# Reordering the seam between attention and experts in a fused audio tower, with a small clear on Pool between scatters

## The chip, the cores and the metric

The kernel runs on one core of a Trainium2 chip. The metric is the device time of one execution in microseconds (us). Before the change it is 282.87 us, the median of three runs (281.76 to 283.83).

Engines are named as the profile does: PE (TensorE, with PEld for its weight loads), DVE (VectorE), ACT (ScalarE), POOL (GpSimd), and SP, which only starts DMAs here. Each has its own instruction stream; they wait for one another through counting semaphores.

## The reference

Input is 32 sequences of 125 frames with 23 features. Four stages follow, all in float32 (N = 32 x 121 = 3872 tokens of 128 features):

```python
h = tdnn(x)                      # windows of 5 frames, linear to 128, relu, batch norm over all tokens
h = h + attention(layernorm(h))  # 8 heads of 16, per sequence, with a column bias from an edge list
n = layernorm(h)
e = argmax(n @ Wr + br)          # one of 8 experts per token (top 1, so its gate is 1)
out = h + relu(n @ W1[e] + b1[e]) @ W2[e] + b2[e]    # 128 -> 512 -> 128
```

## The kernel before, in words

Attention is a software pipeline over sequences b = 0 to 31, one step t per sequence (`for t in range(B)`), then five more steps t = 32 to 36 (`for t in range(B, STEPS)`) in which the last sequences drain while the first five expert tiles already run. The order is written out by hand, once for each engine. In step t:

- PE computes the scores of t (`scores`), the turned scores of t-1 (`scores_T`), the weighted values of t-2 (`weigh`), turns results (`turn`, `turn_back`) and projects the output of t-4 (`output`).
- ACT takes the exponent of t-1, copies sums and turned tiles (`turned_copy`, `sums_copy`), and scales rows of t-5 (`scaled_rows`, it sets `s_x2`).
- DVE reduces the row maxima, divides (`divided(t-3)`), adds the first residual and squares (`first_sublayer(t-4)`).
- POOL computes the second norm's factor (`rstd2(t-4)`) and, after every fourth sequence, the router's logits (`logits`).

Sequences are grouped by four (g = 0 to 7; group six is sequences 24 to 27). For each group DVE finds each token's expert (`experts`), PE ranks the tokens within their expert (`rank_rows`, small bf16 products into a corner of a PSUM bank named by `rank_bank`), and DVE picks each token's place in the region of its expert (`rows_picked`, `row_places`, which sets `r_pos`; `expert_seen` carries the counts on). Then POOL scatters the 121 rows of each sequence to a DRAM buffer, with an indirect DMA (`scatter_rows(b)`, line 435). `scatter_step(b)` says in which step.

The expert part works on 38 tiles of 128 rows, each of one expert. The first 11 tiles (NT1) hold rows of the first 20 sequences, the other 27 need all rows. SP loads a tile from DRAM (`load_rows`), PE transposes it (`transpose_rows`), ACT copies it (`xgT_copy`, line 564) and copies the expert's W1 next to it (`W1_copy`, line 557), PE makes the first product (`ffn_first`, line 1246), ACT and DVE each make half of the hidden layer (`relu` 572, `ffn_relu` 883), PE the second product (`ffn_second`, line 1236), DVE adds the residual (`finish_rows`, line 873, sets `f_y`), and POOL scatters the tile's rows to the output with an indirect DMA (`scatter_out(s)`, line 442). The first seven of these wait for a tile six further on (`f_y >= s + 7`), and there is one `pool.drain()` after the output of tile 24.

Places that the change touches, by line: `scatter_step` 244, `rank_bank` 258, `scatter_out` 438, POOL's loops 466 to 483, ACT's `W1_copy(0)` behind its loop, DVE's steps 32 to 36, PE's `transpose_rows(0)` and `rank_rows(NG - 2)` there.

Of the kernel before, what the change touches and what calls it, by code (L numbers as in the profile page):

```python
# [15 lines left out]
B, TF, DI = 32, 125, 23  # L16
# [18 lines left out]
NT = (N + E * 127) // 128  # L35
# [7 lines left out]
NG = len(GROUPS)  # L43
# [5 lines left out]
def build(nc, x, tok_W, tok_b, gamma, beta, edge_index, edge_attr, q_w, q_b, k_w, k_b, v_w, v_b, o_w, o_b,  # L49
          eb_w, eb_b, Wr, br, W1, b1, W2, b2, out):  # L50
    with ExitStack() as ctx:
        def sb(name, shape, dt=F32):
            return ctx.enter_context(nc.sbuf_tensor(name, shape, dt))
# [135 lines left out]
        mask = sb("mask", [128, NT], I32)  # L189
        sidx = sb("sidx", [128, NT], I32)  # L190

        xg = sb("xg", [128, RING, ROW])
        xgT = sb("xgT", [128, 2, 128])
        W1_tile = sb("W1_tile", [128, 2, F])
# [49 lines left out]
        def scatter_step(b):  # L244
            g = next(n for n, (b0, nb) in enumerate(GROUPS) if b0 <= b < b0 + nb)
            first, i = ranked(g) + 1, b - GROUPS[g][0]
            return first + (i if first < B else i // 2)

        def has(t, back, n=B):

# [6 lines left out]

        def rank_bank(g):

            return psO if g < NG - 1 else psU  # L260

        def score_half(turned):

# [58 lines left out]
        def _(pool):  # L322
# [108 lines left out]
            def scatter_rows(b):  # L431
                g = next(n for n, (b0, nb) in enumerate(GROUPS) if b0 <= b < b0 + nb)
                pool.wait_ge(r_pos, g + 1)
                pool.wait_ge(s_x2, b + 1)
                pool.indirect_dma_start(region_d, bass.IndirectOffsetOnAxis(pos[0:L, b:b + 1], 0), rows[0:L, b, E:E + ROW], None,  # L435
                                        bounds_check=E * CAP - 1, oob_is_err=False).then_inc(d_early if b < B1 else d_rows, 16)

            def scatter_out(s):
                u = s % RING
                pool.wait_ge(f_si, s + 1)  # L440
                pool.wait_ge(f_y, s + 1)
                pool.indirect_dma_start(out, bass.IndirectOffsetOnAxis(sidx[:, s:s + 1], 0), y_out[:, u, :], None,  # L442
                                        bounds_check=N - 1, oob_is_err=False).then_inc(f_sca[u], 16)

            pool.wait_ge(s_rowid, 1)
            pool.wait_ge(l_rows, 16 * N_ROWS)
# [18 lines left out]
                    rstd2(t - 4)  # L465
            for t in range(B, STEPS):
                if t == B + 3:
                    for b in range(done, B - 6):
                        scatter_rows(b)
                    done = B - 6  # L470
                if has(t, 4):
                    rstd2(t - 4)
                while done < B and scatter_step(done) <= t:
                    scatter_rows(done)
                    done += 1
            for b in range(done, B):
                scatter_rows(b)
            for s in range(NT):
                if s < ALONG + 2:
                    pool.wait_ge(f_y, s + 7)  # L480
                scatter_out(s)
                if s == NT - 14:
                    pool.drain()
# [3 lines left out]
        def _(act):  # L487
# [65 lines left out]
            def W1_copy(s):  # L553
                e = act.value_load(eid[0:1, s:s + 1], min_val=0, max_val=E - 1)
                if s >= 2:
                    act.wait_ge(f_L1, s - 1)
                act.activation(W1_tile[:, s % 2, :], W1_sb[:, bass.ds(e * F, F)], ACT.Identity).then_inc(f_w1, 1)  # L557
                tile_expert[s % 2] = e
# [38 lines left out]
            def turned_copy(b):  # L597

                act.wait_ge(s_OT, b + 1)
                act.activation(oT[:, :], psO[:, 256:256 + L], ACT.Identity).then_inc(s_oT, 1)  # L600
# [22 lines left out]
            for t in range(B):  # L623
                p, even = t // 2, t % 2 == 0
                if t == 0:
                    xT_copy(1, psO)
                if not even and p + 1 < NP:
                    q_copy(p + 1, psB[:, 0, :])
                if even and p > 0 and p + 3 < NP:
                    batch_norm(p + 3)  # L630
                if has(t, 4):
                    turned_copy(t - 4)
                if even:
                    v_copy(p, psB[:, 0, :])
                if has(t, 1):
                    exponent(t - 1)
                if has(t, 2):
                    sums_copy(t - 2)
                if even and p + 3 < NP:
                    h0_copy(p + 3, psB[:, 1, :])  # L640
                if not even and p + 2 < NP:
                    xT_copy(p + 2, psB[:, 1, :])
                if has(t, 5):
                    scaled_rows(t - 5)
                if t == B - 3:
                    act.wait_ge(f_b1, 1)
                    act.activation(b1T[:, :], psB[:, 1, 0:E * FC], ACT.Identity).then_inc(f_b1T, 1)
# [4 lines left out]
            sums_copy(B - 2)  # L652
            scaled_rows(B - 5)
            xgT_copy(1)
            act.wait_ge(r_eid, 1)
            act.wait_ge(l_ffn, 48)
            W1_copy(0)
            for t in range(B, STEPS):
                s = t - B
                if s > 0:  # L660
# [21 lines left out]
        def _(dve):  # L682
# [139 lines left out]
            def rows_picked(g):  # L822

                b0, nb = GROUPS[g]
                dve.wait_ge(r_rank, g + 1)
                dve.tensor_tensor(picked_row[0:L, 0:nb, :], rank_bank(g)[0:L, 384:384 + nb * E].rearrange("p (b e) -> p b e", e=E),
                                  oh_bf[0:L, b0:b0 + nb, :], ALU.mult).then_inc(r_pick, 1)

            def row_places(g):

                b0, nb = GROUPS[g]
                dve.wait_ge(r_pick, g + 1)
                with nc.allow_low_precision("whole numbers"):
                    dve.tensor_reduce(pos[0:L, b0:b0 + nb], picked_row[0:L, 0:nb, :], AX.X, ALU.add).then_inc(r_pos, 1)
# [74 lines left out]
            def experts(g):  # L909

                expert_max(g)
                expert_rank(g)
                expert_onehot(g)
# [72 lines left out]
            for t in range(B, STEPS):  # L986
                s = t - B
                if has(t, 3):
                    dve.wait_ge(s_P, t - 3)
                    divided(t - 3)  # L990
                if t == B + 2:
                    rows_picked(NG - 2)
                    row_places(NG - 2)
                if t == B + 3:
                    dve.wait_ge(s_P, B)
                if has(t, 4):
                    first_sublayer(t - 4)
                if t == B + 4:
                    experts(NG - 1)
                ffn_relu(s, e)  # L1000
                e_next = tile_expert(s + 1)
                if t == B + 2:
                    expert_seen(NG - 2)
                if t == B + 4:
                    expert_seen(NG - 1)
                    rows_picked(NG - 1)
                    row_places(NG - 1)
                ffn_resid(s, e)
                if s > 0:
                    finish_rows(s - 1)  # L1010
                if t == B:
                    experts(NG - 2)
                e = e_next

            def rest_tiles():
# [54 lines left out]
        def _(pe):  # L1070
# [193 lines left out]
            def turn(b):  # L1264

                pe.wait_ge(s_on, b + 1)
                pe.transpose(psO[:, 256:256 + L], on[0:L, :], ident[0:L, 0:L]).then_inc(s_OT, 1)  # L1267
# [25 lines left out]
            for t in range(B):  # L1293
# [68 lines left out]
                if t == B - 1:  # L1362
                    pe.wait_ge(s_kT, NP)
                    pe.wait_ge(s_qs, 2 * NP)
                    pe.wait_ge(s_Vs, NP)
                    transpose_rows(0)

            pe.wait_ge(s_exp, B - 1)
            pe.wait_ge(s_qm, B)
            scores_T(B - 1)  # L1370
            pe.wait_ge(s_OTs, B - 2)
            turn(B - 4)
            pe.wait_ge(s_h1, B - 4)
# [11 lines left out]
            for t in range(B + 1, STEPS):  # L1385
                s = t - B
                e = tile_expert(s - 1)
                if has(t, 3):
                    pe.wait_ge(s_h1, t - 4)
                    pe.wait_ge(s_on, t - 3)  # L1390
                    turn_back(t - 3)
                    output(t - 4)
                if has(t, 2):
                    weigh(t - 2)
                if t == B + 2:
                    pe.wait_ge(s_oT, B - 1)
                    pe.wait_ge(s_OTs, B)
                    rank_rows(NG - 2)
                pe.wait_ge(f_xT, s + 1)
                transpose_rows(s + 1)  # L1400
                if t == B + 3:
                    pe.wait_ge(s_h1, B - 1)
                    pe.wait_ge(s_on, B)
                    output(B - 1)
                ffn_first(s)
                if has(t, 3):
                    if t == B + 2:
                        pe.wait_ge(r_pick, NG - 1)
                    pe.wait_ge(s_OTs, min(t - 1, B))
                    turn(t - 3)  # L1410
                ffn_second(s - 1, e)

            pe.wait_ge(s_h1, B)
# [47 lines left out]
```

## Time and profile before

| | |
|---|---|
| median of three runs | 282.87 us (281.76 to 283.83) |
| the profiled execution | 282.8 us, span 281.1 us |
| PE busy | 247.3 us, 88% of the span |
| DVE, ACT, POOL busy | 180.9, 165.8, 145.6 us |
| mean granted clock of TensorE | 0.951 of full |
| indirect DMAs to the region (L435) | 32, 1083 ns each on POOL |
| indirect DMAs to the output (L442) | 38, 980 ns each on POOL |

The span is measured inside the execution; the other 1.7 us lie around it. A busy indirect DMA on POOL is the time in which POOL makes its descriptors, not the transfer. "Remote", or "another core or an unknown queue" in the chain of waits, stands where an engine started again and the trace shows nothing that released it.

### The profile page before, as it was taken

The numbers are of one execution on the slowest core, as the hardware profiler recorded it, in microseconds if no ns is written. First come the engines' busy times: TensorE is split into PE (matmuls) and PEld (weight loads), VectorE is DVE, ScalarE is ACT, GpSimd is POOL, SyncE is SP. The second block draws the span as 40 slices with busy tenths as digits, with TensorE's granted clock in tenths as the row PEclk, the third lists the DMA queues.
The fourth block names the chain that finished last, engine by engine and source line by source line (L and its number), as shares of the span: only waits on it lengthen the run. The fifth ranks groups of instructions, "written<-read, shape, count | busy, mean of one in ns | idle before, by whom it ended". The sixth has DMA issues, their size and how long they took to land.

```text
span 281.1 us, 8987 instructions
## 1 busy us (share of the span) xinstructions
PE 247.3 (88%) x2852; PEld 207.9 (74%) x2852; DVE 180.9 (64%) x679; ACT 165.8 (59%) x405; POOL 145.6 (52%) x275
## 2 busy tenths in 40 slices
PE   3999689999999999999998986975969559999693
PEld 3855466888887777878776755965969559999693
DVE  3896555678888788787788864663825225564352
ACT  3873355687676776766765664553536226776460
POOL 8001733344587776777776434475143744443444
PEclk9999999999999999999999997799798958999899
DMA  3110599000010111010110135123045423330000
GB/s 114 38 43 0 150 338 266 3 2 2 2 39 20 38 39 37 21 38 20 38 39 25 30 98 151 39 56 89 2 139 144 124 59 89 97 88 21 27 22 0
DMA packets 14462, 18.20 MB, mean 65 GB/s; under 512 B 3992, under 2 KB 10556, under 8 KB 14417
## 3 DMA queue, kind: packets, MB, share of 16 engines
q1 hardware_dynamic: 10976, 11.23, 14.1%
q0 software_dynamic: 3296, 6.00, 7.3%
q8 instruction: 24, 0.39, 0.6%
q10 hardware_dynamic: 144, 0.41, 0.4%
q14 instruction: 22, 0.17, 0.2%
HBM read 10.58 MB, written 7.54 MB: 64 GB/s over the span
## 4 chain that ended last, share of the span: by engine, by line
PE 67%; DVE 8%; issue 7%; another core or an unknown queue 6%; ACT 5%; POOL 3%; DMA 2%; ACTq 2%; POOLq 1%; SPq 0%; DVEq 0%
PE psS L1246 11%; PE psB L1146 9%; PE psS L1162 6%; PE psB L1236 5%; PE psO L1289 5%; PE psS L1172 4%; PE psO L1236 3%; PE psB L1130 3%; PE psU L1279 2%; DVE nmax L944 2%; PE psO L1267 2%; PE psU L1273 2%; PE psB L1152 2%; PE psB L1223 2%
## 5 line engine op out<-in xcount | busy, mean ns | idle before, releaser
L442 POOL DMA_INDIRECT out<-y_out,sidx x38 | 37.3, 980 | 47.1 <-DVE y_out L873 21.9
L1246 PE MATMUL psS<-xgT,W_tile 128*128 128x128 f32 x304 | 45.8, 300 | 2.7 <-ACT W_tile L557 2.6
L883 DVE TENSOR_SCALAR hT<-psS,b1T 128x128 f32<-128x128 f32 x76 | 23.3, 346 | 37.2 <-PE psS L1246 26.0
L944 DVE TENSOR_REDUCE nmax<-psS 121x8 f32<-121x968 f32 x32 | 37.2, 1164 | 14.6 <-PE psS L1172 13.2
L1246 PEld LDWEIGHTS psS<-xgT,W_tile 128*128 128x128 f32 x304 | 42.1, 214 | 3.3 <-issue 1.9
L609 ACT ACTIVATE PT<-psS 121x968 f32<-121x968 f32 x32 | 31.3, 978 | 17.3 <-DVE nmax L944 14.0
L572 ACT ACTIVATE hT<-psS,b1T 128x128 f32<-128x128 f32 x76 | 23.9, 364 | 29.5 <-PE psS L1246 21.3
L435 POOL DMA_INDIRECT region_d<-rows,pos x32 | 34.7, 1083 | 11.7 <-issue 11.4
L557 ACT ACTIVATE W_tile<-W_sb 128x512 f32 x38 | 23.9, 630 | 6.4 <-issue 3.7
L1236 PE MATMUL psB<-W_sb,hT 128*128 x168 | 25.6, 302 | 1.4 <-issue 1.4
L1236 PEld LDWEIGHTS psB<-W_sb,hT 128*128 128x128 f32 x168 | 23.7, 218 | 1.9 <-issue 1.7
L1162 PE MATMUL psS<-kT,qT 32*121 32x121 f32 x512 | 22.3, 288 | 1.3 <-ACT PT L609 0.7
L1236 PE MATMUL psO<-W_sb,hT 128*128 x136 | 19.5, 289 | 4.3 <-issue 4.1
L1162 PEld LDWEIGHTS psS<-kT,qT 32*121 32x121 f32 x512 | 16.5, 179 | 8.7 <-issue 6.2
L1236 PEld LDWEIGHTS psO<-W_sb,hT 128*128 128x128 f32 x136 | 17.6, 202 | 5.1 <-issue 5.0
L614 ACT ACTIVATE OTs<-psO 128x242 f32<-128x242 f32 x32 | 11.9, 373 | 14.2 <-PE psO L1289 13.8
L1289 PE MATMUL psO<-PT,V 121*32 121x121 f32 x512 | 20.3, 277 | 0.0
L422 POOL TENSOR_SCALAR var<-ss 121x1 f32<-121x1 f32 x32 | 6.1, 192 | 26.3 <-DVE sq L936 21.8
L1223 PE MATMUL psB<-ident,xg 128*128 128x128 f32 x38 | 11.4, 301 | 9.3 <-ACT xgT L564 7.2
L1172 PE MATMUL psS<-qm,kT 32*121 32x121 f32 x512 | 19.5, 265 | 0.0
L426 POOL TENSOR_TENSOR rs<-var,minus_half 121x1 f32<-121x1 f32 x32 | 18.0, 563 | 2.7
L957 DVE TENSOR_TENSOR qm<-qT,psU 128x242 f32<-128x242 f32 x32 | 12.9, 403 | 9.0 <-PE psU L1342 9.0
(261 smaller groups left out, 545.0 us busy)
## 6 DMA issues: line engine op xcount, KB each, us to landing
xg<-region_d SPq DMA_DIRECT2D x38, 129.0 KB
W_sb<-in_L_ffn_W SPq DMA_DIRECT2D x1, 2048.0 KB, 9.8
region_d<-pads SPq DMA_DIRECT2D x1, 1032.0 KB, 6.7
out<-y_out,sidx POOLq DMA_INDIRECT x38
b_bc<-in_L_ffn_b SPq DMA_DIRECT2D x1, 512.0 KB, 5.1
region_d<-rows,pos POOLq DMA_INDIRECT x32
xs<-in_x ACTq DMA_DIRECT2D x1, 402.5 KB, 3.5
edge_i<-in_L_attn_edge_index SPq DMA_DIRECT2D x1, 64.0 KB, 3.8
```

Source lines behind the costliest of these rows:

```text
L435: pool.indirect_dma_start(region_d, bass.IndirectOffsetOnAxis(pos[0:L, b:b + 1], 0), rows[0:L, b, E:E + ROW], None, bounds_check=E * CAP - ...
L442: pool.indirect_dma_start(out, bass.IndirectOffsetOnAxis(sidx[:, s:s + 1], 0), y_out[:, u, :], None, bounds_check=N - 1, oob_is_err=False) ...
L557: act.activation(W1_tile[:, s % 2, :], W1_sb[:, bass.ds(e * F, F)], ACT.Identity).then_inc(f_w1, 1)
L572: ins = act.activation(hT[:, s % 2, c * 128:(c + 1) * 128], psS[:, s % 2, c * 128:(c + 1) * 128], ACT.Relu, bias=b1T[:, bass.ds(e * FC + c ...
L609: act.activation(PT[0:L, b % 2, :, :, :], score_half(1), ACT.Exp).then_inc(s_exp, 1)
L944: dve.tensor_reduce(nmax[0:L, :].rearrange("p (j c) -> p j c", c=HB)[:, :, HD + 1:HD + 3], score_half(0), AX.X, ALU.max, negate=True).then ...
L1146: return pe.matmul(bank[:, g * PL:(g + 1) * PL], w[:, g * 128:(g + 1) * 128], xT[:, p % 2, :], start=True, stop=True)
L1162: ins = pe.matmul(psS[0:L, j, a * 128:a * 128 + L], qT[rws, p % 2, a, n0:n0 + L], kT[rws, p % 2, a, n0:n0 + L], start=True, stop=True)
L1172: ins = pe.matmul(psS[0:L, j, 256 + a * 128:256 + a * 128 + L], kT[rws, p % 2, a, n0:n0 + L], qm[rws, a, :], start=True, stop=True)
L1236: ins = pe.matmul(tile_out(s), hT[:, s % 2, c * 128:(c + 1) * 128], W2_sb[:, bass.ds(e * F + c * D, D)], start=(c == 0), stop=(c == FC - 1))
L1246: ins = pe.matmul(psS[:, c // 2 * 2 + s % 2, c % 2 * 128:(c % 2 + 1) * 128], W1_tile[:, s % 2, c * 128:(c + 1) * 128], xgT[:, s % 2, :], s ...
L1289: ins = pe.matmul(psO[j * HB:(j + 1) * HB, a * 128:a * 128 + L], V[0:L, b // 2 % 2, b % 2, a * HG + j, :], PT[0:L, b % 2, j, a, :], start= ...
```

## The change

POOL:

- `scatter_step` gives two rows per step also to a group that begins in step 30, so that sequences 20 and 21 are scattered in step 30, and 22 and 23 in step 31 (before: 20 to 23 in steps 30 to 33).
- Sequences 24, 25 and 26 are scattered in steps 33, 34 and 35 by explicit calls (before: 24 and 25 in step 35, 26 and 27 in step 36). 27 to 31 follow behind the loop (before: 28 to 31).
- A new tile `pause` of 43 columns. Behind each scatter of sequences 27 to 31, and each scatter to the output but for the last three tiles, POOL clears one column of it with a memset. Nothing reads it.

Group six, a step forward: DVE's `experts` and `expert_seen` stand in step 32 ahead of the first tile's hidden layer, its picks in step 33; PE's `rank_rows` in step 33 without its two waits, in the bank of the tiles' second products; the wait for the pick stands ahead of the second product of tile 0.

ACT copies the first tile's W1 in step 31. PE transposes the first tile behind the last turned scores.

```diff
+        pause = sb("pause", [128, NT + 5])
...
-            return first + (i if first < B else i // 2)
+            return first + (i if first < B - 2 else i // 2)
...
-            return psO if g < NG - 1 else psU
+            return psO[:, :] if g < NG - 2 else psB[:, 1, :] if g == NG - 2 else psU[:, :]
...
                 pool.indirect_dma_start(out, ...
+                if s < NT - 3:
+                    pool.memset(pause[:, s:s + 1], 0.0)
...
             for t in range(B, STEPS):
                 if t == B + 3:
-                    for b in range(done, B - 6):
-                        scatter_rows(b)
-                    done = B - 6
+                    scatter_rows(B - 6)
+                    done = B - 5
                 if has(t, 4):
                     rstd2(t - 4)
-                while done < B and scatter_step(done) <= t:
-                    scatter_rows(done)
-                    done += 1
+                if t == B + 1:
+                    scatter_rows(B - 8)
+                if t == B + 2:
+                    scatter_rows(B - 7)
+                    done = B - 6
             for b in range(done, B):
                 scatter_rows(b)
+                pool.memset(pause[:, NT + b - (B - 5):NT + b - (B - 5) + 1], 0.0)
...   (ACT, step B - 1, behind turned_copy)
+                if t == B - 1:
+                    act.wait_ge(r_eid, 1)
+                    act.wait_ge(l_ffn, 48)
+                    W1_copy(0)
...
             xgT_copy(1)
-            act.wait_ge(r_eid, 1)
-            act.wait_ge(l_ffn, 48)
-            W1_copy(0)
...   (DVE, steps B to B + 4)
-                if t == B + 2:
-                    rows_picked(NG - 2)
-                    row_places(NG - 2)
...
                     first_sublayer(t - 4)
+                if t == B:
+                    experts(NG - 2)
+                    expert_seen(NG - 2)
+                if t == B + 1:
+                    rows_picked(NG - 2)
+                    row_places(NG - 2)
...
-                if t == B + 2:
-                    expert_seen(NG - 2)
...
-                if t == B:
-                    experts(NG - 2)
...   (PE)
-                    transpose_rows(0)
...
             scores_T(B - 1)
+            transpose_rows(0)
...
-                if t == B + 2:
-                    pe.wait_ge(s_oT, B - 1)
-                    pe.wait_ge(s_OTs, B)
+                if t == B + 1:
                     rank_rows(NG - 2)
...
                 if has(t, 3):
-                    if t == B + 2:
-                        pe.wait_ge(r_pick, NG - 1)
                     pe.wait_ge(s_OTs, min(t - 1, B))
                     turn(t - 3)
+                if t == B + 1:
+                    pe.wait_ge(r_pick, NG - 1)
                 ffn_second(s - 1, e)
```

## Rows read from the trace of the kernel before

**Rows 1.** The page's strip of TensorE's granted clock, 40 equal slices, tenths.
```profile
PEclk9999999999999999999999997799798958999899
```

**Rows 2.** The chain of waits from 150 us: start us, us, what.
```profile
223.88 4.83 another core or an unknown queue
...
261.96 2.02 another core or an unknown queue
```

**Rows 3.** The timeline, steps 31 and 32: start us, us, engine line operation [idle before].
```profile
164.55 0.98 ACT L609 ACTIVATE PT<-psS 121x968 f32<-121x968 f32 x1 [0.95 <-DVE nmax L944]
...
169.68 0.63 ACT L557 ACTIVATE W_tile<-W_sb 128x512 f32 x1 [0.34 <-issue]
...
170.45 1.13 PE L1246 MATMUL psS<-xgT,W_tile 128*128 128x128 f32 x8 [1.75 <-ACT W_tile L557]
...
173.33 0.18 DVE L791 TENSOR_REDUCE top<-lg 121x4 f32<-121x32 f32 x1
```

**Rows 4.** Busy time by stretch: engines' busy us, then granted clock, DMA share, GB/s.
```profile
172.50:179.00 6.50, 6.44 (x40) 5.81 (x41) 3.83 (x19) 3.01 (x9) 1.85 (x3) 0.50 0.46 116
193.30:196.00 2.70, 0.00 (x0) 0.00 (x1) 0.39 (x3) 0.39 (x2) 1.19 (x2) 1.00 0.35 96
196.00:199.80 3.80, 3.77 (x18) 3.65 (x19) 2.91 (x21) 2.48 (x7) 0.00 (x0) 0.55 0.01 4
...
264.40:267.90 3.50, 3.47 (x17) 3.50 (x18) 2.08 (x9) 2.23 (x7) 1.95 (x2) 0.51 0.03 9
```

**Rows 5.** The timeline, the scatters of sequences 26 to 31, first and last.
```profile
186.93 1.09 POOL L435 DMA_INDIRECT region_d<-rows,pos  x1 [0.64 <-issue]
...
190.82 0.27 PE L1223 MATMUL psB<-ident,xg 128*128 128x128 f32 x1
...
193.78 1.02 POOL L435 DMA_INDIRECT region_d<-rows,pos  x1 [0.31 <-issue]
...
195.61 0.28 ACT L564 ACTIVATE xgT<-psB 128x128 f32<-128x128 f32 x1 [2.72 <-remote]
```

**Rows 6.** The timeline, around the second of two output scatters (the first starts at 202.36).
```profile
203.00 1.06 PE L1236 MATMUL psB<-W_sb,hT 128*128 x8
...
203.78 0.98 POOL L442 DMA_INDIRECT out<-y_out,sidx  x1 [0.31 <-issue]
...
205.25 0.29 DVE L873 TENSOR_TENSOR y_out<-psB,resid 128x128 f32<-128x128 f32 x1 [0.59 <-PE psB L1236]
```

**Rows 7.** The timeline, eight output scatters in a row, first and last.
```profile
217.28 0.97 POOL L442 DMA_INDIRECT out<-y_out,sidx  x1 [1.01 <-issue]
...
219.70 0.27 PE L1223 MATMUL psB<-ident,xg 128*128 128x128 f32 x1
...
226.23 0.97 POOL L442 DMA_INDIRECT out<-y_out,sidx  x1 [0.30 <-issue]
...
228.72 0.28 ACT L564 ACTIVATE xgT<-psB 128x128 f32<-128x128 f32 x1 [4.26 <-remote]
```

**Rows 8.** The timeline, later scatters: paced, the five behind the drain, the last.
```profile
240.38 0.97 POOL L442 DMA_INDIRECT out<-y_out,sidx  x1 [0.92 <-issue]
...
256.73 0.97 POOL L442 DMA_INDIRECT out<-y_out,sidx  x1 [5.68 <-DVE y_out L873]
...
261.84 1.12 POOL L442 DMA_INDIRECT out<-y_out,sidx  x1 [0.31 <-issue]
...
264.01 0.28 ACT L564 ACTIVATE xgT<-psB 128x128 f32<-128x128 f32 x1 [1.46 <-remote]
...
278.18 0.97 POOL L442 DMA_INDIRECT out<-y_out,sidx  x1 [0.31 <-issue]
```

**Rows 9.** The timeline: compute on POOL behind a scatter; by line: a memset.
```profile
168.65 1.09 POOL L435 DMA_INDIRECT region_d<-rows,pos  x1 [0.69 <-issue]
169.78 0.21 POOL L422 TENSOR_SCALAR var<-ss 121x1 f32<-121x1 f32 x1
...
L368 POOL MEMSET early_to<- 128x1 f32 x1 | 0.1, 89 | 0.0
```

## The prediction, made before the changed kernel had run

> **What bounds the kernel now.** I read the strips of the page first. TensorE is busy nine tenths or more in most slices, but its clock strip falls in three places, around 174, 230 and 266 us [rows 1]. Then the chain of waits, from 160 us on: some of its longest pieces belong to no engine at all, as 4.83 and 2.02 us of "another core or an unknown queue" [rows 2]. These are not DMA loads. The timeline shows what they are. TensorE starts a transposition at 190.82 and ends it at 191.09; ScalarE's copy of it, which waits for that and has a free engine, starts at 195.61 [rows 5]. The same at 219.70 against 228.72 [rows 7]. So TensorE's work was done and the news of it came 4.5 and 8.8 us late, while TensorE sat idle with the next tile.
>
> What else runs in these stretches is the same each time: POOL issues indirect transfers without a gap. There are six from 186.93 to 194.80 [rows 5], eight from 217.28 to 227.20 [rows 7], and five from 256.73 to 262.96 [rows 8]. One start to the next is 0.97+0.31 = 1.28 us there. Where POOL is paced by the tiles, 0.97+0.92 = 1.89 us apart [rows 8], nothing is late. Even two in a row hold something up: the product that ended at 204.06 lets VectorE go only at 205.25 [rows 6]. I call these stretches the first, second and third **jam**. The freeing comes after the last transfer's end by 0.49 us for 2 transfers [rows 6], 1.05 for 5 [rows 8], 1.52 for 8 [rows 7], some 0.17 more for each. An estimate from that: something behind POOL needs about 1.28+0.17 = 1.45 us per transfer, and falls behind when they come each 1.28. It is a reading of four points, and the first jam (0.77 for 6, spaced a little wider) fits it [rows 5].
>
> **The change, part by part.** The sum is made against the profiled execution, 282.8 us (span 281.1), which is 0.1 under the median of 282.87.
>
> 1. First copy of W1 in step 31. Now ScalarE copies it at 169.68 and TensorE waits 1.75 us for it before the first expert product [rows 3]. In step 31 ScalarE waits 0.95 us before its exponent at 164.55; the copy takes 0.63 and its register load some tenths, so it fits there but for about 0.2 [rows 3]. The expert ids are there by then, since the loads that use them have started. Gain 1.7; between 0 (ScalarE late) and 1.9.
>
> 2. The clock. After this wait it drops to half, and 6.50 us from 172.5 to 179 run at 0.50 with TensorE busy 6.44 [rows 4]. If the product starts 1.7 us earlier the hole ahead of the drop closes. At full clock the 6.44 us would be 3.2, of which ScalarE's and VectorE's turns take back a part: I take 2.0, with 0 and 3.2 as ends.
>
> 3. Group six a step forward. TensorE gets its five small bf16 products in step 33 in place of 34, in another bank; VectorE gets the five expert operations (0.2 us each, from 173.33 [rows 3]) before the first hidden layer instead of after it, and two picks in step 33. They move and add nothing. The wait for the pick now stands before the first second-layer product; behind it on TensorE stands all of step 34, but VectorE can pick as soon as the ranks are made, while TensorE makes a whole first product (1.13 us, [rows 3]), so it finds the pick done. Cost 0; from -0.5 to +1.0 (the five operations in front of the first hidden layer). The first transposition of a tile goes behind the last turned scores: ScalarE's copy then comes later, ahead of an exponent that waits for the same scores anyway. 0, within 0.3.
>
> 4. Rows moved on POOL. Rows 21 to 23 go earlier, 24, 25, 26 in steps 33, 34, 35. Still two transfers stand before the last norm of step 35, which is as late as now: 0. Behind the loop five are left instead of six, and the last four must wait for the last ranks, so a new run starts with four.
>
> 5. The cleared column: 0.09 us on POOL, and compute starts 0.04 after a transfer's end (169.74 to 169.78) [rows 9]. A transfer to the next goes from 1.28 to about 1.41 us. Below, it cannot be nothing; above, the nearest row is a transfer that starts 0.69 after compute (instead of 0.31), so 1.79 us [rows 9]. I take 1.41, as the shorter gap is the rule. POOL has 1.89 per tile [rows 8], so outside runs this is hidden. Inside a run the backlog then grows by 1.45-1.41 = 0.04 us per transfer instead of 0.17, so some four intervals go by before it is where one interval brings it now.
>  - First jam, a run of four: gone. Gain 2.7 of idle TensorE and half of 3.77 at clock 0.55, 1.8 [rows 4]: 4.5.
>  - Second jam: it starts from a backlog of seven tiles, because the first seven outputs wait for tiles six ahead. The jam comes a few transfers later and lasts as long, until POOL has caught up. Nine transfers by 0.13: cost 1.2.
>  - Third jam, five transfers behind the drain: the 2.02 us of the chain [rows 2] and half of 3.47 at 0.51 [rows 4], 3.8 in all. The run is about as long as the threshold: half of it, 1.9.
>
> Sum: 282.8-1.7-2.0-4.5+1.2-1.9 = **273.9 us**.
>
> The page SBUF — State Buffer of the Trainium skill, section Who interferes with whom, says that only the port pair shared by VectorE and GpSimd causes contention; its table names nobody with whom TensorE's or ScalarE's ports are shared. By it no spacing on POOL could free ScalarE earlier than 195.61 or 228.72; the trace disagrees at least so far that ScalarE waited with its input ready. By that rule the sum would be the first rival's.
>
> **Rivals.**
> A. *The pause is too short.* In the first run six transfers start (193.78-186.93)/5 = 1.37 us apart and jam [rows 5]; 1.41 is hardly more, and still under 1.45. Then all jams stay and last longer: 282.8-1.7-2.0+1.2+0.5 = 280.8; without the clock's part 282.8. Chance 0.27, three quarters of it within 1%.
> B. *The pause ends all jams.* Any other instruction between two transfers lets the backlog out. Then the second run of transfers starts at 217.28-8.2 = 209.1 and POOL itself sets the end: 31 more by 1.41 and 5.4 us for the drain [rows 8] bring the last to 258 against 278.2 now [rows 8], so 263. For it: in the attention steps, where compute stands between transfers, nothing is late. Against: there they are also further apart. Chance 0.17.
> C. *Slower: POOL becomes the bound.* If the clearing has to wait until the transfer before it has really gone, as the drain does (5.68 us of idle POOL at 256.73, of which some 5.4 are more than the 0.30 of others [rows 8]), every output transfer takes that along. It decides from where 31 transfers and the drain fill the present 60.9 us from 217.28 to 278.18 [rows 7, 8]: a spacing of (60.9-5.4)/31 = 1.79 us. At 2.1, say, it is 65.1+5.4 = 70.5, 9.6 more, less parts 1 and 2: 288.7. Against it: compute starts 0.04 us behind a transfer [rows 9]. Chance 0.12.
> D. *Parts 1 and 2 give nothing* since ScalarE or VectorE is late in step 31 to 33, and jams are eased by little: 282. Chance 0.08.
>
> The page GPSIMD Engine Reference of the Trainium skill, section Instruction dispatch, says that an instruction's completion does not hold back the next Pool instruction. By it rival C would not be; the 0.04 us agrees.
>
> **Numbers.** The forecast has 0.36, and is likelier than each rival. Its own range is 270 to 277, from the ends of parts 1 to 3 and of the third jam. About 1% (2.8 us) is what a measurement of this kernel can tell from no change. Faster by more: forecast, B and a quarter of A, 0.36+0.17+0.07 = 0.60. Within: the rest of A and D, 0.20+0.08 = 0.28. Slower: C, 0.12. The range for 8 in 10 goes from 264 to 283, leaving out C and a part of B.
>
> **What would show it.** Part 1: no wait for the W1 copy before the first expert product, its start near 168.8. Part 2: no stretch at clock 0.50 behind it. Part 3: the ranks of group six in the step of expert tile 1, and no gap before the product behind the wait for the pick. Part 5: MEMSET rows of 0.09 us between transfers, starts 1.41 apart; no "another core or an unknown queue" in the run of the last four rows; a jam in the outputs of tiles 7 to 20. The forecast is wrong if the first jam is still there with 1.41 us (A), if the second is gone (B), or if transfers are 1.8 us apart or more and POOL is never idle (C).

## The result: 1.1% faster, about a third of the forecast

| | before | after |
|---|---|---|
| median of four runs each | 283.35 us (281.76 to 284.36) | 279.93 us (278.58 to 280.81) |
| ratio, with its 95% interval | | 0.9894 [0.9847, 0.9940] |
| profiled execution, span | 282.8, 281.1 us | 280.24, 278.5 us |

The forecast was 8.9 us less and 3.4 us were measured. Its direction was right and its size wrong. Rival A (the pause too short, all jams stay, 280.8) came nearest.

Here and below a median is over all executions of a kernel, while a ratio leaves out those that ran over 1.5% above its fastest (one, with 128 columns, took 560.62 us).

### The profile after

The strip of the granted clock and the group of output scatters, from the page of the changed kernel (busy us, mean ns; idle us before them):
```profile
PEclk9997999999999999999999995999999958999888
...
L443 POOL DMA_INDIRECT out<-y_out,sidx x38 | 37.4, 985 | 41.4 <-DVE y_out L879 20.1
```
The strip falls around 170, 226 and 260 us and behind that. Before, it also had a 7 at 197 to 204 us, behind the first jam, and an 8 at 211 to 218 [rows 1]; both are gone. Behind the other two jams it is no better.

The timeline of POOL in the changed kernel, the run of the last four row scatters (sequences 28 to 31) with the one of 27 ahead of it, and what waited on ScalarE:
```profile
185.73 1.09 POOL L436 DMA_INDIRECT region_d<-rows,pos  x1 [0.64 <-issue]
186.83 0.11 POOL L482 MEMSET pause<- 128x1 f32 x1
188.62 1.02 POOL L436 DMA_INDIRECT region_d<-rows,pos  x1 [1.68 <-DVE pos L840]
189.65 0.11 POOL L482 MEMSET pause<- 128x1 f32 x1
189.95 1.02 POOL L436 DMA_INDIRECT region_d<-rows,pos  x1 [0.19 <-issue]
...
192.59 1.03 POOL L436 DMA_INDIRECT region_d<-rows,pos  x1 [0.19 <-issue]
...
194.42 0.63 ACT L577 ACTIVATE hT<-psS,b1T 128x128 f32<-128x128 f32 x2 [4.23 <-remote]
```
The same view of the output scatters, nine in a row, first, second and last:
```profile
212.84 0.97 POOL L443 DMA_INDIRECT out<-y_out,sidx  x1 [1.60 <-DVE y_out L879]
213.80 0.12 POOL L446 MEMSET pause<- 128x1 f32 x1
214.12 0.97 POOL L443 DMA_INDIRECT out<-y_out,sidx  x1 [0.19 <-issue]
...
223.07 0.97 POOL L443 DMA_INDIRECT out<-y_out,sidx  x1 [0.19 <-issue]
...
225.82 0.63 ACT L577 ACTIVATE hT<-psS,b1T 128x128 f32<-128x128 f32 x2 [5.57 <-remote]
```
This is the reading that matters. The MEMSET is there, with 0.12 us, but the next scatter has 0.19 us of idle time before it where it had 0.30 [rows 7]. 0.12 and 0.19 are the old 0.31: the clear stands inside time that POOL took from one scatter to the next anyway. Starts are (223.07-212.84)/8 = 1.28 us apart, as before. ScalarE's release still trails the run: 225.82-224.04 = 1.78 us behind the last of nine. The prediction's points (0.49 for 2, 1.05 for 5, 1.52 for 8) lie near 0.15+0.17n, which gives 1.68 for nine.

One reading of the prediction needs a correction. Of the 4.5 and 8.8 us by which it has ScalarE's two copies late, ScalarE spent a part on earlier work in its own order. Just before them it stood idle 2.72 us [rows 5] and 4.26 us [rows 7].

The chain of waits, first of the changed kernel, all its pieces of this kind from 188 us on, then those pieces of the kernel before that [rows 2] left out:
```profile
189.94 4.36 another core or an unknown queue
...
214.51 5.44 another core or an unknown queue
...
220.00 5.70 another core or an unknown queue
...
255.75 1.95 another core or an unknown queue
...
258.64 2.71 another core or an unknown queue
```
```profile
188.83 2.35 another core or an unknown queue
...
192.30 3.28 another core or an unknown queue
...
218.79 4.15 another core or an unknown queue
```
Their sums are 20.2 us after and 2.35+3.28+4.15+4.83+2.02 = 16.6 before. By these pieces the first jam is shorter (4.36 for 5.63) and the other two are longer.

To see where the time was won, I measure landmarks from the start of the exponent of sequence 27, since what lies ahead of it moved by up to 3.8 us between profiled executions, of kernels that are alike there. "Late places" is the last of the three small products in which TensorE hands on the places of the late tiles (line 1431 of the kernel before); their loads wait for it. From the timelines, in us:

| from the exponent of sequence 27 to | before | early copy alone | early copy and pair | after without clears | after | after, pair undone |
|---|---|---|---|---|---|---|
| first expert product | 17.9 | 16.0 | 17.1 | 18.6 | 18.6 | 16.4 |
| ranks of group seven | 35.1 | 31.2 | 33.5 | 33.3 | 33.3 | 31.2 |
| late places | 48.4 | 44.6 | 47.6 | 43.6 | 44.3 | 41.9 |
| output scatter 6 | 64.7 | 58.8 | 62.2 | 58.8 | 59.7 | 57.2 |
| last output scatter | 125.6 | 121.2 | 124.9 | 122.4 | 122.5 | 119.8 |

The changed kernel is 1.8 us ahead of the kernel before at the ranks, 4.1 at the late places, behind the first jam, and 5.0 at output scatter 6. Behind that, where the second and third jam lie, it loses 1.9 again.

### The profile page after: what moved, and what is told of

Its sections match the earlier page's. It is cut to its first block, busy times and chain, and to the rows that moved or that the text cites. A ratio compares the mean times of both kernels' runs of the same rounds, so it can differ in the third digit from the quotient of the medians.

```text
span 278.5 us, 9025 instructions
## 1 busy us (share of the span) xinstructions
PE 245.8 (88%) x2852; PEld 205.5 (74%) x2852; DVE 180.6 (65%) x679; ACT 164.9 (59%) x405; POOL 150.1 (54%) x315
## 4 chain that ended last, share of the span: by engine, by line
PE 63%; issue 11%; another core or an unknown queue 7%; DVE 6%; POOL 6%; ACT 4%; DMA 1%; ACTq 1%; POOLq 1%; DVEq 0%
PE psB L1151 9%; PE psS L1251 8%; PE psS L1167 6%; PE psB L1241 5%; PE psO L1294 5%; PE psS L1177 4%; PE psO L1241 3%; PE psB L1135 3%; POOL region_d L436 3%; DVE nmax L950 2%; PE psS L1147 2%; PE psO L1272 2%; PE psU L1284 2%; PE psB L1157 2%
## 5 line engine op out<-in xcount | busy, mean ns | idle before, releaser
L1251 PE MATMUL psS<-xgT,W_tile 128*128 128x128 f32 x304 | 43.1, 288 | 0.8 <-ACT W_tile L562 0.6
L1251 PEld LDWEIGHTS psS<-xgT,W_tile 128*128 128x128 f32 x304 | 39.4, 202 | 1.6 <-ACT W_tile L562 1.3
L1241 PE MATMUL psB<-W_sb,hT 128*128 x168 | 24.5, 293 | 8.6 <-ACT hT L577 7.7
L1241 PEld LDWEIGHTS psB<-W_sb,hT 128*128 128x128 f32 x168 | 22.0, 205 | 9.4 <-issue 9.3
L1177 PE MATMUL psS<-qm,kT 32*121 32x121 f32 x512 | 20.1, 269 | 0.8 <-ACT PT L614 0.8
L1177 PEld LDWEIGHTS psS<-qm,kT 32*121 32x121 f32 x512 | 17.2, 185 | 1.1 <-issue 1.1
```

The costliest lines, as they stand in the source:

```text
L1177: ins = pe.matmul(psS[0:L, j, 256 + a * 128:256 + a * 128 + L], kT[rws, p % 2, a, n0:n0 + L], qm[rws, a, :], start=True, stop=True)
L1241: ins = pe.matmul(tile_out(s), hT[:, s % 2, c * 128:(c + 1) * 128], W2_sb[:, bass.ds(e * F + c * D, D)], start=(c == 0), stop=(c == FC - 1))
L1251: ins = pe.matmul(psS[:, c // 2 * 2 + s % 2, c % 2 * 128:(c % 2 + 1) * 128], W1_tile[:, s % 2, c * 128:(c + 1) * 128], xgT[:, s % 2, :], s ...
```

## Experiments

Each ratio is against the kernel before, on the same chip, with its 95% interval. The theory at the start: the clear of one column widens nothing, and the gain is parts 1 and 2 and nothing else. Rival: the clears did ease something, and the moved rows pay too.

### The clears, taken out and put in alone

```
-                    pool.memset(pause[:, s:s + 1], 0.0)
-                pool.memset(pause[:, NT + b - (B - 5):NT + b - (B - 5) + 1], 0.0)
```
The changed kernel without its clears:

> The changed kernel without any cleared column; all else as changed. Theory (my new one): the clear of 0.1 us fits into the 0.31 us that POOL takes between two scatters anyway (1.28 us start to start with and without it), so it does nothing: 280 us, within 0.5% of the changed kernel, jams as long as there. Rival (the forecast): the clears ease the jams, so taking them out loses at least 2 us: 282 or more.

The kernel before with the two clears, and nothing else:

> The kernel before, plus only the clears: behind the scatters of sequences 28 to 31 and each output scatter but the last three. Theory: nothing, 283.3 within 0.5%, scatters still 1.28 us apart in runs. Rival (the clears give the whole gain): 280.

Measured: without clears 281.16 us, 0.9913 [0.9841, 0.9986]; clears alone 283.85 us, 1.0027 [0.9964, 1.0090]. The landmarks of the changed kernel agree with and without them to 0.1 us at the ranks and at the last scatter (between these the one without is up to 0.9 us sooner). Part 5 of the change does nothing that these runs can tell.

### How wide must the pause be

The clear is made wider, with a semaphore of its own and eight areas in turn:
```
-        pause = sb("pause", [128, NT + 5])
+        pause = sb("pause", [128, 8, 256])
+        s_clear = sem("s_clear")
...
+            def clear():
+                k = cleared[0]
+                if k >= 8:
+                    pool.wait_ge(s_clear, k - 7)
+                pool.memset(pause[:, k % 8, :], 0.0).then_inc(s_clear, 1)
+                cleared[0] = k + 1
```
256 columns, and then 128 and 480:

> The changed kernel with a clear of 256 columns (0.30 us by the memsets at the kernel's start) in the place of one column; eight areas in turn with a semaphore of their own. Theory (a scatter needs about 1.45 us behind POOL; the jam comes from a shorter spacing): the spacing becomes 0.97+0.03+0.30+0.2 to 0.3 = 1.50 to 1.60 us, above 1.45, and the jams go or shrink to one scatter: TensorE idle of some 12 us and its half clock behind it go, 265 to 272. Rival (the jam comes from POOL having many scatters in a row, whatever the spacing): jams stay and last longer by 0.25 per scatter, 281 to 284.

> The changed kernel with clears of 128 columns. By the clear of 256 columns (0.33 us busy, output scatters 1.46 us apart, jams cut to about a third) I expect 0.23 us and 1.36 us apart. Theory (what is behind POOL needs about 1.45 us per scatter): 1.36 is still too short, the jams stay in length, 279 to 281. Rival (any visible gap helps in proportion): half way between one column and 256, 277.5 to 278.5.

> The changed kernel with clears of 480 columns: 0.51 us busy, output scatters 1.65 us apart, still under the 1.89 us of a tile. Theory: no piece of the chain without an engine is left over 1 us in the runs of scatters; the backlog of outputs is worked off slowly beside the tiles: 268 to 273, under the 275.8 of 256 columns. Rival (the last gain of 256 columns was all there is, and POOL's longer work sets the end): 276 or more.

And 384 columns, not behind the last eight outputs (`if s < NT - 8`):

> The changed kernel with clears of 384 columns (0.43 us busy, 1.56 us apart) behind each output scatter but the last eight. With 480 columns TensorE was done at 259.8 and POOL's last scatter started at 265.4: POOL set the end. Theory: 1.56 is above 1.45, so still no jams, and POOL ends some 3 to 5 us sooner: 266 to 269. Rival (jams come back under 1.65): 272 or more.

| columns | clear, us | output scatters apart, us | time, us | ratio | TensorE busy in 16 us, at what clock | unnamed pieces of the chain, us |
|---|---|---|---|---|---|---|
| 1 (after) | 0.12 | 1.28 | 279.93 | 0.9894 [0.9847, 0.9940] | 7.07, 0.80 | 4.36, 5.44, 5.70, 1.95, 2.71 |
| 128 | 0.23 | 1.36 | 280.60 | 0.9880 [0.9846, 0.9915] | 7.71, 0.74 | 6.55, 2.09 |
| 256 | 0.33 | 1.46 | 275.79 | 0.9747 [0.9687, 0.9806] | 10.67, 0.73 | 0.19, 2.79, 1.37, 1.44 |
| 384 | 0.44 | 1.57 | 272.89 | 0.9670 [0.9594, 0.9746] | 14.82, 0.99 | 1.44, 1.55, 0.63, 1.45, 0.67, 1.07 |
| 480 | 0.52 | 1.65 | 271.38 | 0.9583 [0.9510, 0.9657] | 15.25, 1.00 | none |

The 16 us lie around the long run of output scatters (from 212, 213 and then three times from 206 us on). They are the better measure. The unnamed pieces are those of "another core or an unknown queue". They miss jams that stand under a named wait, as the first with 128 columns, where ScalarE is idle 3.61 us before 195.17. With 384 columns TensorE is at work during most of them, and with 480 the chain runs along POOL from 206 us on.

The timeline of POOL in the kernel with 480 columns:
```profile
206.22 0.97 POOL L453 DMA_INDIRECT out<-y_out,sidx  x1 [2.50 <-DVE y_out L889]
207.19 0.52 POOL L439 MEMSET pause<- 128x480 f32 x1
207.87 0.97 POOL L453 DMA_INDIRECT out<-y_out,sidx  x1 [0.17 <-issue]
```
Busy time by stretch, the 16 us around the long run of output scatters, one core's engines in the order PE, PEld, DVE, ACT, POOL, then granted clock, DMA share, GB/s: of the kernel before, of the changed one and of the one with 480 columns:
```profile
214.00:230.00 16.00, 9.79 (x74) 9.34 (x73) 4.46 (x20) 6.03 (x17) 9.21 (x11) 0.80 0.39 115
```
```profile
212.00:228.00 16.00, 7.07 (x54) 6.67 (x54) 4.49 (x20) 4.91 (x16) 9.94 (x19) 0.80 0.32 94
```
```profile
206.00:222.00 16.00, 15.25 (x130) 14.54 (x129) 8.76 (x38) 10.54 (x30) 14.29 (x19) 1.00 0.53 144
```
TensorE is busy 15.25 of 16 us instead of 7.07, though POOL works more. So the theory of the jams stood: the wider spacing removes them. Its threshold of 1.45 us stood only roughly. At 1.36 us the time is no better, at 1.46 about half of the gain is there (4.1 of 8.5 us, where 265 to 272 us were expected), at 1.57 most of it (7.0; 266 to 269 were expected). The semaphore of the wide clears is not what helps, since the one of 128 columns has it too. Only the pause was not there in the change. With 480 columns TensorE is done at 259.8 and POOL at 266.39; the end is POOL's.

The same clears on other bases: in the kernel before alone, and behind the outputs only.

> The kernel before with clears of 480 columns behind its last four row scatters and each output scatter but the last three, and no other part of the change. Theory (a jam is a matter of the spacing of scatters): its second and third jam are gone, the first (six rows, of which only the last four are spaced) is shorter; the same 8 to 9 us as on the changed kernel (280 to 271.4) are gained: 273 to 276. Rival (the wide clear needs the other parts, since the first jam hides the reload): less than 4 us, 279 or more.

> The changed kernel with clears of 480 columns behind output scatters only, none between the rows. The row run of four then stands 1.32 us apart and TensorE waits some 2.65 us in it, as in the changed kernel. Theory: the first jam is back, but since POOL set the end with 480 columns (TensorE done 5.6 us before it), a part of it is covered: 271 to 274. Rival (the first jam is paid in full): 274 to 276.

Measured: 274.76 us, 0.9620 [0.9572, 0.9669], and 272.59 us, 0.9634 [0.9585, 0.9682]. The spacing alone gives 3.8%; the other parts add nothing to it that these intervals resolve. Most of it comes from the outputs' spacing. Whether POOL has to be busy in that time, or could as well stand still, was not tried.

### The early copy of W1

Alone in the kernel before:
```
+                if t == B - 1:
+                    act.wait_ge(r_eid, 1)
+                    act.wait_ge(l_ffn, 48)
+                    W1_copy(0)
...
-            act.wait_ge(r_eid, 1)
-            act.wait_ge(l_ffn, 48)
-            W1_copy(0)
```


> The kernel before with the first copy of W1 in step 31 and nothing else. There POOL has one scatter in step 30, so the pair of row scatters is not there that delays ScalarE in step 31 of the changed kernel. Part 1 of the prediction: TensorE's 1.75 us wait goes, 1 to 2 us gained, 281.5 to 282.5. Rival (the copy delays the exponent of sequence 30 and the turned scores by as much as it saves): no change, 283.5, and the first expert product no earlier.

Measured: 280.23 us (12 runs), 0.9913 [0.9872, 0.9954]. The timeline around the first expert product of this kernel, and the stretch of its columns:
```profile
164.84 0.63 ACT L557 ACTIVATE W_tile<-W_sb 128x512 f32 x1 [0.95 <-issue]
165.38 0.96 ACT L609 ACTIVATE PT<-psS 121x968 f32<-121x968 f32 x1
...
168.85 1.06 PE L1247 MATMUL psS<-xgT,W_tile 128*128 128x128 f32 x8
```
```profile
174.00:176.00 2.00, 1.99 (x18) 1.83 (x19) 1.49 (x8) 1.19 (x3) 1.45 (x3) 1.00 0.35 102
176.00:178.00 2.00, 2.00 (x20) 1.94 (x19) 1.80 (x10) 1.01 (x4) 0.90 (x3) 1.00 0.60 151
```
The copy stands in the 0.95 us that ScalarE had free and pushes the exponent back by 0.5 (0.2 were thought), the product has no wait before it, and the clock stays at 2.4 GHz where it was at 1.2 [rows 4]. The product is 1.9 us sooner and the ranks 3.9: there parts 1 and 2 gave what they were put at, 3.7. In the time it is 2.6 us, more than the 1 to 2 expected of the run.

The reverse, the changed kernel with the copy behind the loop again:

> The changed kernel with the first copy of W1 behind the loop again. In the changed kernel this copy stands before the exponent of sequence 30, which starts 0.55 us after what it waited for. Theory: the early copy gains nothing, since TensorE loses in step 31 what it saves at the first expert product: 280 within 0.5%. Rival (part 1 of the prediction): 1.7 us slower, 281.6.

Measured: 283.26 us, 0.9936 [0.9845, 1.0028]. By the ratios this is 0.4% slower than the changed kernel, and the intervals overlap widely; it says nothing alone.

### The moved steps

The changed kernel without clears and with group six where it was. Against the kernel before, it has the early copy, the first transposition a little later, and the scatters in pairs (rows 20 and 21 in step 30, 22 and 23 behind them):
```
-            return first + (i if first < B else i // 2)
+            return first + (i if first < B - 2 else i // 2)
...
-                    transpose_rows(0)
...
             scores_T(B - 1)
+            transpose_rows(0)
```


> The changed kernel without clears and with group six where it was: its experts behind tile 0, its ranks in step 34, rows 24 and 25 in step 35, 26 and 27 in step 36; rows 20 to 23 two per step and the early W1 copy stay. The same kernel with group six forward and without clears gave 0.991 of before. Theory (group six's step forward, with rows 24 to 26 earlier, is what shortens the last run of row scatters from six to four and is the gain): 282 to 283.5, no gain left. Rival (the gain is in the W1 copy): 280.

The changed kernel with rows 20 to 23 one per step, as before:
```
-            return first + (i if first < B - 2 else i // 2)
+            return first + (i if first < B else i // 2)
```


> The changed kernel with rows 20 to 23 again one per step from step 30 (22 in step 32, 23 and 24 in step 33). Theory: the pair of scatters in step 30 (1.39 us apart) is a small jam of its own, it holds ScalarE's turned copy 0.7 us in step 31; without it the first expert product starts 0.7 to 1.3 us sooner and the whole is 0 to 1.5 us faster, 278.5 to 280. Rival (two rows per step help, since POOL is freer later): 1 us slower, 281.

Measured: 282.79 us (12 runs), 1.0011 [0.9972, 1.0050], and 279.97 us (6 runs), 0.9885 [0.9825, 0.9946]. The first is the telling one: it has the early copy and yet has lost all of its gain, 2.6 us against the run with the copy alone. What differs from that run are the pairs and the one transposition. It is the pairs: with them undone and the transposition left, the ranks come at 31.2 us, as with the copy alone. The timeline of the changed kernel shows how:
```profile
161.54 1.09 POOL L436 DMA_INDIRECT region_d<-rows,pos  x1 [0.32 <-issue]
162.94 1.02 POOL L436 DMA_INDIRECT region_d<-rows,pos  x1 [0.30 <-issue]
163.61 0.29 PE L1272 MATMUL psO<-ident,on 121*128 121x121 f32 x1
164.64 0.27 ACT L605 ACTIVATE oT<-psO 128x121 f32<-128x121 f32 x1 [1.16 <-PE psO L1272]
...
167.62 1.18 PE L1177 MATMUL psS<-qm,kT 32*121 32x121 f32 x16 [0.84 <-ACT PT L614]
```
and the stretches behind it, first of the changed kernel, then of the one with one scatter per step, which is some 2 us ahead of it there in its landmarks:
```profile
168.00:170.00 2.00, 2.00 (x21) 1.55 (x18) 0.00 (x0) 0.76 (x3) 1.05 (x4) 0.50 0.49 120
172.00:174.00 2.00, 1.86 (x9) 1.47 (x8) 1.19 (x7) 1.03 (x4) 1.18 (x3) 0.54 0.73 198
174.00:176.00 2.00, 1.79 (x26) 1.32 (x27) 1.70 (x8) 1.46 (x5) 0.00 (x0) 1.00 0.47 121
```
```profile
174.00:176.00 2.00, 1.13 (x13) 0.84 (x17) 1.69 (x9) 1.86 (x7) 1.60 (x2) 1.00 0.64 176
176.00:178.00 2.00, 2.00 (x33) 1.81 (x26) 1.27 (x8) 0.65 (x2) 0.76 (x2) 1.00 0.53 147
```
Two scatters without a gap are a small jam, as [rows 6] had shown for outputs: the transposition that ended at 163.90 lets ScalarE go at 164.64, 0.74 us late, where one scatter per step leaves 0.04. TensorE has a hole of 0.84 us behind it, the clock is at 0.50 from 168 to 170 and at 0.54 from 172 to 174, where with one per step it stays at 1.00, and the ranks come 2.1 us later. So the pair brings back the low clock that part 1 had taken away, some 4 us further forward.

Group six forward, with what it lets the last four scatters do, gives this back: the landmarks of the changed kernel without clears stand 4.0 us sooner than in the kernel with group six where it was at the late places, and 2.4 at the last scatter. In the changed kernel VectorE's count of all tiles stands ahead of the first jam:
```profile
190.01 0.15 DVE L1024 TENSOR_SCALAR all_t<-psU 128x8 int32<-128x8 f32 x1
```
In the kernel before, that operation ran at 195.78, behind its jam, and with group six back at 194.49. The places of the late tiles, and so their loads, hang on it.

There is a second difference. TensorE still has its hole in the first jam (2.65 us before 195.32 in the changed kernel, 2.73 before 196.03 in the kernel before), but the clock behind it does not fall. The 3.8 us behind it, in the changed kernel, then the 3.9 us in the kernel with group six where it was:
```profile
195.40:199.20 3.80, 3.17 (x28) 2.96 (x29) 3.24 (x19) 2.94 (x9) 0.00 (x0) 1.00 0.01 2
```
```profile
194.70:198.60 3.90, 3.12 (x17) 2.96 (x18) 2.98 (x22) 2.48 (x7) 0.00 (x0) 0.74 0.01 4
```
In the kernel before it was 0.55 [rows 4]. Without clears it is 1.00 too, so the clears are not the reason. How the gain divides between the earlier count and the clock, and why the clock stays up, was not separated.

With the pair undone in the changed kernel the last scatter is 2.6 us sooner in its landmarks, but the medians (279.97 and 279.93) do not show it. Its profiled execution was the slowest of its six (280.84) and had 3.2 us more ahead of the exponent of sequence 27; whether that comes with the edit or by chance is open.

### The wait of the outputs, and the drain

The first seven outputs not held back:
```
-                if s < ALONG + 2:
-                    pool.wait_ge(f_y, s + 7)
```


> The changed kernel in which the first seven output scatters don't wait for a tile six further on. Theory: the backlog of seven tiles behind the second jam is gone, but the first outputs now follow the last row scatters with no pause, so that the first jam grows by what is ready then (some five tiles, 6 us) and lies on the tiles before the reload: 278 to 284, the second jam (5.4 and 5.7 us in the chain) gone. Rival (the backlog is not what makes the second run): the second jam stays as it is.

The changed kernel without the drain:
```
-                if s == NT - 14:
-                    pool.drain()
```


> The changed kernel without the one drain on POOL behind the output of tile 24. Theory: the drain holds POOL 6 us, makes a backlog of four tiles, and this the third jam (pieces of 1.95 and 2.71 us in the chain, half clock behind); without it the third jam is gone and 3 to 5 us are gained: 275 to 277. Rival (the drain spares something else, a wait on POOL that comes anyway): 280 or more.

Measured: 277.50 us, 0.9810 [0.9732, 0.9888], and 280.33 us, 0.9906 [0.9858, 0.9953]. Without the wait the outputs follow the rows at once, one long jam of 4.36+6.31 us in the chain takes the place of the first and second (4.36+5.44+5.70), so it costs less than the two; the interval still touches that of the changed kernel. Without the drain the third jam is gone and the last scatter starts earlier, but the end does not move (275 to 277 us were expected). The last scatter of the kernel without the drain (span 278.3) and of the changed kernel (span 278.5):
```profile
271.26 0.97 POOL L443 DMA_INDIRECT out<-y_out,sidx  x1 [0.30 <-issue]
```
```profile
275.63 0.97 POOL L443 DMA_INDIRECT out<-y_out,sidx  x1 [0.30 <-issue]
```
From its end to the end of the span: 278.3-272.23 = 6.1 us and 278.5-276.60 = 1.9 us. The time of the drain is paid at the end if it is not paid before.

### A better version

One scatter per step for rows 20 to 23, 480 columns but not behind the last eight outputs, and then with the drain behind the output of tile 3 besides:
```
-                if s == NT - 14:
+                if s == 3:
```


> The changed kernel with rows 20 to 23 one per step, clears of 480 columns behind rows 27 to 31 and behind output scatters but the last eight. Theory: 2.2 us sooner at the ranks of group seven, as rowsback was, and about 2 us less of POOL's work behind TensorE's end: 267 to 270, faster than 271.4. Rival (the seam's time is taken up by the reload's wait): 271.

> The same with the drain behind the output of tile 3, where POOL waits some 4 us for tile 10 anyway, instead of tile 24. Theory: POOL no longer stands 6 us in the middle, is never behind at the end, and TensorE sets the end again: 263 to 266. Rival (as without the drain: the 6 us come back behind the last scatter): the same as best480 or slower, with some 6 us between the last scatter and the end in place of 1.9.

Measured: 271.87 us, 0.9611 [0.9564, 0.9658], and **269.30 us**, 0.9519 [0.9463, 0.9575]: 4.8% under the kernel before and 3.8% under the changed one. The first is no better than 480 columns behind all but the last three (271.38), and the interval of the second overlaps that one's too. In the second the last scatter starts at 263.60, ends at 264.57, and the span ends at 267.6, 3.0 us behind that, so with the drain that early a part of its time is paid again. Both were expected to do better (267 to 270 and 263 to 266).

## Why the prediction was wrong, step by step

1. *Early copy*, -1.7: right alone, where it brings the first product 1.9 us forward. In the changed kernel TensorE does not wait for the copy, but the first product comes 0.7 us later than before, for the reason under 4.
2. *Clock*, -2.0: right alone (both together 3.9 against 3.7 at the ranks, 2.6 in the time), not in the changed kernel, where it fell for another reason.
3. *Group six forward*, 0: a miss of size. Each instruction was costed where it stood, but not what comes sooner because of it. With the row scatters' new order it is worth 2.4 us at the last scatter: VectorE's count stands ahead of the jam, and the clock behind the jam stays up.
4. *Rows moved on POOL*, 0: **this failed.** The text looked only at the end of the loop. The move makes a pair in step 30, and the first part of the text had quoted [rows 6] for just what a pair does. It costs 2.1 us at the ranks in the trace and, with the old place of group six, 2.6 us in the time.
5. *The cleared column*, -5.2 in sum: **this failed, and it is most of the error.** The step was "A transfer to the next goes from 1.28 to about 1.41 us. Below, it cannot be nothing". It was nothing. The 0.31 us between two scatters were taken for a gap that stays when something is put in; the clear overlaps it. The row that would have said so was cited for another end: compute that starts 0.04 us behind a scatter [rows 9] says that POOL has nothing to finish in those 0.31. The forecast of the first jam gone (-4.5), and of the third halved (-1.9), rested on this alone, and so did the 1.2 lost in the second. Of the 4.5, the 2.7 us of idle TensorE stayed (2.65). The half clock behind it went, but not by the clears, since it went without them too.

That 3.7 us forecast for parts 1 and 2 and 3.4 measured lie close is chance: at the ranks only 1.8 us of the 3.9 were left, and the rest came from the step that the sum had at 0.

Of the rivals, A had the right place for the error and priced it at 280.8, close to the 279.93 measured. Its reason was off, as it had the pause at 1.41 and too short, with longer jams for it. C, POOL as the bound, did not come with the change, but it did with 480 columns, where POOL ends 6.6 us behind TensorE. B, all jams gone and POOL at the end, put 263; the kernel with a real pause has 271.38. D, parts 1 and 2 giving nothing, is not so for these parts alone.

The page SBUF — State Buffer of the Trainium skill, section Who interferes with whom, names only the port pair of VectorE and GpSimd as contended. By it no spacing on POOL would have freed ScalarE or TensorE sooner. Moving the spacing from 1.28 to 1.65 us took 8.5 us off the time, so the rule does not cover what happens here. The page GPSIMD Engine Reference of the Trainium skill, section Instruction dispatch, says that a Pool instruction is not held back by the completion of the one before. The clear that starts at 213.80, as the scatter before it ends (212.84+0.97), agrees.

**Open.** What it is behind POOL that falls behind at 1.28 us per scatter and not at 1.65 was not found, nor why it is news of TensorE's work that is late by it. Shown is that a clear wide enough to space the scatters removes the jams. Why a drain's 5 us have to be paid once was not tried further.

## What to carry to other kernels

The idle time between two instructions is not a gap that stays: a small instruction put there can vanish in it, so ask of the smallest insertion first whether it moves the next start. If an engine seems to wait for work of another that is long done, look for what a third queue does at that moment, and try its spacing over a range wide enough to see the threshold. And of a moved step ask two things, what it stands beside now, and what comes sooner because of it.

## What the hardware showed that was not expected

- A clear of one column (0.12 us) between two indirect scatters on POOL costs no time: the idle time falls from 0.31 to 0.19 us. Clears of 128, 256, 384 and 480 columns take 0.23, 0.33, 0.44 and 0.52 us, 0.16 to 0.17 us of idle time stay, and the starts go to 1.36, 1.46, 1.57 and 1.65 us.
- In runs of four or more scatters 1.28 to 1.42 us apart, ScalarE stands idle for 1.5 to 6.4 us at a time (1.46 us before 264.01 in the kernel before, 6.42 before 227.68 with 128 columns) although the work of TensorE that it waits for is done for all or most of that time. With 1.65 us between the output scatters TensorE is busy 15.25 of 16 us.
- A hole of about 2.7 us in TensorE's work was followed by a granted clock of 0.55 in the kernel before and of 1.00 in the changed one.
- The drain's time, left out, comes back at the end of the kernel: 6.1 us from the last scatter's end to the end of the span, instead of 1.9.
